# The merge of the odd heads of self blocks issued from ScalarE's queue, and all orders planned from new constants

## The reference

```python
# every block: normalise, modulate by the condition, compute, add to x (some through a gate)
L0: self attention (rope, block mask) -> cross attention (77 context tokens, mask) -> MLP 256-1024-256 (tanh gelu)
L1: cross attention (normalised and modulated context)
L2: self attention -> cross attention (normalised context) -> MLP (tanh gelu)
L3: self attention (rope) -> cross attention (rope) -> MLP (erf gelu)
# attention, 16 heads of 16: softmax(q k^T / 4) v, then the output projection
```

## Time and profile before

| | us |
|---|---|
| median of three executions | 2699.41 (2697.4 to 2700.83) |
| the profiled execution | 2701.83 |
| its span, first to last instruction | 2700.0 |
| PE busy | 2581.8 (96%) |
| DVE busy | 1747.8 (65%) |
| ACT busy | 1445.8 (54%) |
| POOL busy | 667.4 (25%) |
| mean granted clock of TensorE | 0.968 of full |

### The profile page before, as it was taken

One profiled execution on the slowest core, in us unless ns is written; L12 is line 12 of the kernel. 1 busy time (PEld: TensorE's weight loads), 2 busy tenths in 40 slices (PEclk: granted clock), 3 DMA queues, 4 the chain that ended last, 5 costly groups with the idle time before them and its releaser, 6 DMA issues.

```text
span 2700.0 us, 54860 instructions
## 1 busy us (share of the span) xinstructions
PE 2581.8 (96%) x19774; PEld 1869.2 (69%) x19774; DVE 1747.8 (65%) x4179; ACT 1445.8 (54%) x2421; POOL 667.4 (25%) x650
## 2 busy tenths in 40 slices
PE   7789999999999999989999999999999999999987
PEld 5557767677677766656777777777777777777765
DVE  4466666666665556677677767676677666766632
ACT  1235555544545555544566655556565656555642
POOL 2022222222221222212222222223323232324220
PEclk9799999999999988888999999999999999999989
DMA  6343423433433465554443434334335343434310
GB/s 206 101 146 123 128 94 120 133 96 100 139 105 108 132 200 167 167 174 142 132 146 112 144 109 135 119 124 134 118 103 177 101 139 106 144 100 136 105 62 18
DMA packets 297860, 340.55 MB, mean 126 GB/s; under 512 B 72954, under 2 KB 188506, under 8 KB 297020
## 3 DMA queue, kind: packets, MB, share of 16 engines
q1 hardware_dynamic: 264124, 286.68, 34.2%
q10 hardware_dynamic: 33280, 50.35, 5.1%
q0 software_dynamic: 192, 0.01, 0.0%
HBM read 203.42 MB, written 116.21 MB: 118 GB/s over the span
## 4 chain that ended last, share of the span: by engine, by line
PE 79%; DVE 10%; issue 3%; DMA 2%; SPq 1%; POOL 1%; ACT 1%; ACTq 0%; DVEq 0%; POOLq 0%
PE gen L1356 13%; PE gen L1365 12%; PE gen L1252 12%; PE gen L1218 11%; PE gen L1336 11%; PE score L1280 4%; PE score L1265 4%; PE score L1310 4%; DVE row_max L1691 4%; PE score L1294 3%; PE score L1316 3%; PE gen L1227 3%; DVE xhat L1605 1%; DVE x L1742 1%; POOL xnT L1550 1%
## 5 line engine op out<-in xcount | busy, mean ns | idle before, releaser
L1691 DVE TENSOR_REDUCE row_max<-score 128x4 f32<-128x1024 f32 (+1 forms) x640 | 650.6, 1045 | 210.4 <-PE score L1280 130.1
L1508 ACT ACTIVATE probs<-score 128x1024 f32<-128x1024 f32 (+1 forms) x576 | 570.9, 1026 | 369.6 <-PE score L1310 251.9
L1356 PE MATMUL gen<-xnT,w_w1M 128*128 128x256 f32 x1536 | 373.5, 392 | 3.1 <-ACT xnT L1446 2.9
L1365 PE MATMUL gen<-w_w2M,hT 128*128 128x256 f32 x1536 | 355.7, 385 | 3.0 <-ACT hT L1532 2.4
L1365 PEld LDWEIGHTS gen<-w_w2M,hT 128*128 128x128 f32 x1536 | 286.7, 191 | 65.1 <-issue 26.2
L1356 PEld LDWEIGHTS gen<-xnT,w_w1M 128*128 128x128 f32 x1536 | 284.9, 192 | 59.4 <-issue 7.5
L1550 POOL TENSOR_TENSOR xnT<-xnT,xhat 128x512 f32<-128x512 f32 x112 | 148.9, 1330 | 707.0 <-DVE xhat L1720 706.8
L1542 POOL TENSOR_TENSOR rstd<-var_eps,minus_half 128x2 f32<-128x2 f32 x160 | 115.7, 723 | 809.2 <-DVE var_eps L1599 809.0
L1532 ACT ACTIVATE hT<-gen,b_b 128x256 f32<-128x256 f32 x384 | 159.1, 472 | 179.0 <-PE gen L1356 178.0
L1446 ACT ACTIVATE xnT<-gen,mod_all 128x256 f32<-128x256 f32 x288 | 146.8, 569 | 153.7 <-PE gen L1227 151.2
L1336 PE MATMUL gen<-probs,v_self 128*32 128x256 f32 x3072 | 206.3, 386 | 0.5 <-ACT probs L1508 0.5
(11 more groups left out here) (160 smaller groups left out, 4050.4 us busy)
## 6 DMA issues: line engine op xcount, KB each, us to landing
q_stack<-parts_scratch SPq DMA_DIRECT2D x336, 256.0 KB
parts_scratch<-parts ACTq DMA_DIRECT2D x160, 256.0 KB, 2.5
parts_scratch<-parts SPq DMA_DIRECT2D x160, 256.0 KB, 2.3
k_self<-parts_scratch SPq DMA_DIRECT2D x144, 256.0 KB, 4.1
k_cross<-parts_scratch SPq DMA_DIRECT2D x192, 78.0 KB, 2.5
x_scratch<-x SPq DMA_DIRECT2D x48, 256.0 KB, 3.2
x_in<-x_scratch SPq DMA_DIRECT2D x48, 256.0 KB, 2.8
gate<-gates_scratch SPq DMA_DIRECT2D x80, 128.0 KB, 3.2
```

The costliest lines, as they stand in the source:

```text
L1356: mm = pe.matmul(buf[:, i * S:i * S + S], w["M"]["w1"][:, fc, col:col + P], xnT[s][:, fc, :], start=fc == 0, stop=fc == FC - 1)
L1365: mm = pe.matmul(buf[:, 0:D], hT[:, j, c * P:c * P + P], w["M"]["w2"][:, j, :], start=j == 0, stop=j == FFC - 1)
L1508: act.activation(probs[st.probs][0:keys, :, :], score[st.fill.buf][0:keys, :, :].rearrange("p a (r q) -> p (a r) q", r=2), ACT.Exp, bias=k ...
L1691: dve.tensor_reduce(dst, src, AX_X, ALU.max).then_inc(max_done[b], 1)
```

## The change

Two things. In self blocks too, `sh` becomes a step of ACT; the function that issued it from SP is gone. And 39 names instead of 33 have a bonus in `FIRST`, nearly all with other values; STAY is 4.1. Costs, rings, slots, arithmetic and the bytes moved stay as they are, and every engine's list is written anew by the same `run`.

```diff
-FIRST = {"S": 2.5, "ce": 15.3, "cl": 4.2, "dv": -3.6, "ex": -5.2, "ge": 15.3, "hi": 20.3, "ldc": 19.7, "ldg": 17.0, "ldx": 10.1, "lh": -6.3, "ln": -6.6, "lo": 8.1, "mr": 2.3, "mx": 5.7, "out": 3.8, "ph": -2.2, "pv": -6.6, "pw": 6.0, "qkv": -6.1, "res": -10.1, "rp": -1.8, "rt": -6.9, "sd": 9.4, "sg": -3.1, "sh": 10.2, "sm": 4.1, "stx": 6.3, "up": -0.1, "ve": -10.0, "xT": -2.5, "xb": -13.1, "xe": 8.4, "zq": 6.6}
-MARGIN, AGE, STAY = 1.38, 15.7, 4
+FIRST = {"S": 3.5, "ST": -0.1, "cT": -3.1, "ce": 17.4, "cl": 1.0, "dv": -1.2, "ex": 2.0, "ge": 23.1, "hi": 16.1, "ldc": 36.5, "ldg": 24.4, "ldx": 12.3, "lh": -24.9, "ll": -7.8, "ln": -18.0, "lo": -3.9, "mr": 3.0, "mx": -6.7, "nm": -10.1, "nx": 11.3, "out": 3.8, "ph": -2.2, "pv": -2.0, "pw": -5.3, "qkv": -6.0, "res": -16.5, "rp": 30.4, "rs": -2.3, "rt": -6.9, "sd": 23.1, "sg": 13.4, "sh": 8.7, "sm": -2.7, "stx": 16.5, "up": -0.1, "ve": -11.8, "xT": -2.5, "xb": -24.1, "xe": 8.4, "zq": 8.9}
+MARGIN, AGE, STAY = 1.38, 15.7, 4.1
...
-            placed.append(add("sh", h, "sp" if blk.whole else "act", [pv]))
+            placed.append(add("sh", h, "act", [pv]))
...
-                def place_heads(st):
-                    s, h, buf = st.slot, st.j, of(st, "pv", st.j).buf
-                    sp.wait_ge(*moved(of(st, "pv", h).fill))
-                    sp.dma_start(atT[s][1:P:2, h, :], oT[buf][1:P:2, 0, :]).then_inc(heads_placed[buf], 16)
...
-                    elif st.name == "sh":
-                        place_heads(st)
```

## The result

The changed kernel is slower: 2709.61 us in the median of nine executions (2694.7 to 2717.67), against 2695.43 (2685.19 to 2703.84) for the kernel before on the same chip. The medians lie 14.2 us apart; the ratio, which is estimated over all executions and so isn't exactly the quotient of the medians, is 1.0048, 95% interval [1.0033, 1.0063]. So 13 to 14 us are lost, where 13.5 were forecast to be won. The time lies inside the range of 2662 to 2711, near its upper end; it is rival (c)'s time. The profiled execution took 2717.55 us (span 2715.7, clock 0.967). PE is busy as long as before, 2582.6 us against 2581.8; what grew is its idle time, from 118.2 to 133.1 us. (The clock of the profiled execution before is 0.968.)

A forecast was written before the change was run, and what follows sets the result against it. PE (96% busy) was taken as the bound, with 160 us of idle time and lost clock to draw on. Terms -1 -2 -7 -4 -3 = -17, less a 3.5 discount, gave -13.5: 2686 us, range 2662 to 2711.

The forecast's parts named there:

- rival (c): L1 stretch: DVE's new list holds back `ln`, `res`, `lo`, `mx` behind maxima; slower, 2711 us; chance 22%.
- Part 1: Self blocks' `sh` issued from ACT: waits move to the gather, little gained; -1 us, between -3.5 and +8.
- Part 2, full stretches: 240 to 860 and 1320 to 2580 us: 10 fewer breaks in matmul runs; -2 us, 12 either way.
- Part 2, the L1 stretch: 860 to 1320 us: maxima earlier in DVE's list free score banks sooner; -7 us, bounds -30 and +20.
- Part 2, the start: Pipeline fill: a third of two stalls, 7.81 and 4.15 us, goes, with lost clock; -4 us, bounds -15 and +10.
- Part 2, the end: Last jobs: half a chance that `out` goes ahead of the previous job's `down`; -3 us, bounds -8 and +6.
- The discount: A quarter off the L1, start and end terms, since re-ordered lists can open new gaps; +3.5 us.

The follow-up runs named there:

- e1: The kernel before with only the 96 `sh` of self blocks moved from SP's list to ACT's, directly behind their `pv`: 2703.51 us, ratio 1.0015.
- e8: The kernel before with the last `out` ahead of job 62's two `down` and L2's first weight load 60 places later on SP: 2699.67 us, ratio 1.0002.
- e14: The changed kernel with DVE's job 17 statistics behind job 12's residual and SP's last MLP weight load behind job 52's loads: 2701.17 us, ratio 1.0004.

## Why the prediction was wrong

The sign was wrong, the size that of rival (c). Step by step:

**Part 1 (-1): right in what it described, its price not resolved.** The waits moved as said: L1119 grew by 124.8 us where L1125 had had 116.5. The landing is 2.0 us on ACT's queue. By time, e1's interval [0.9999, 1.0030] holds everything from -0.3 to +8 us; no wait of PE for an `ex` behind an `sh` was found. At one clock e1 stands at +4.8, inside the stated -3.5 to +8; the other three pairs don't repeat it. The Trainium skill's rule ("DMA: Bandwidth & Descriptors", "Issuing engines are not separate DMA queues") that another issuer saves only issue time fits: no gain was resolved in any of the four pairs.

**Part 2, full stretches (-2, within 12): this step failed, its bound just held.** By equal work the stretches of this step, with the edge from L2 to L3 that lies in the second, are 11.8 us longer (+7, -6, +6.6 and +4). L2 is 6 us shorter, since six waits of 0.66 to 0.69 us for row maxima and two for `xhat` (1.9 us) in the 8 idle us of the earlier trace rows are gone; L0 is 7 longer, mostly by the eight waits in front of score tiles (10.6 us), and L3 4 longer, in part by small gaps before `down`. The step took it that what other engines do is worth nothing there, because PE had only 14.7 idle us. That bounds a gain and not a loss. Breaks, on which it was built, hardly changed: 1776 changes of tiling in PE's list, 1774 before. How much of L0's +7 is real stays open, as said above; no edit took it away.

**Part 2, the L1 stretch (-7): this step failed, and it is the one that the experiments bear on.** It priced the stretch from 860 to 1320 as one, by PE's waits for maxima, and took half of a hoped-for gain. The maxima's three rows grew from 17.4 to 20.7 us. L1 and the edge before it are 5.8 us longer together: the edge is longer by 10.7, L1 shorter by 5. Rival (c) named the mechanism, a DVE list that holds back `res`, but put it in all sixteen jobs and behind maxima, at 4.8 us a job. The runs show it once, behind the context statistics of a job five ahead, in a wait of 5.9 us where it was 3.1, plus the clock. That rival (c)'s time came out is therefore luck in part. Which constant put the statistics in front is not shown: `res` went from -10.1 to -16.5 and `cl` from 4.2 to 1.0, but the walk with `res` alone put back to -10.1 still has them in front. The step's sum had no term for a level's edge, where the next jobs' first loads and the last residuals meet.

**Part 2, the start (-4): nothing.** The 7.81 us stall is 7.62 and the fill as long as before.

**Part 2, the end (-3): right.** The half chance came true: `out` of job 63 is ahead of the `down` of job 62, and the last `up` takes 7.17 instead of 9.65. It brings 2 us by equal work, and e8 says that so little isn't seen in the time.

**Missed: the edge from L2 to L3 (+6.6).** A weight load issued just ahead of the store and the loads of a job's keys. The prediction took nothing off or on for SP's order there. The profile shows this cause; that it costs time by itself no run shows, and with the order mended PE waits 3.36 us for the weights instead.

**The discount.** A quarter off for lists that fall differently was too little, and it could only shrink a gain. Of 160 us of idle time and clock the forecast took what could be won, and weighed what an order could lose only in its bounds.

## What to carry to other kernels

When all lists are planned anew, look at the places where one phase hands over to the next before summing terms over stretches: there steps of far-apart jobs stand next to each other, and one that waits for a load, put ahead of one whose data is there, made a wait of 5.9 us out of one of 3.1. In a planned list, keep a step that only prepares a later job behind the residual that frees a bank. A bulk load just ahead of a store that is waited for is worth avoiding too, though here its price in time is not shown. To mend a list, move single steps in the finished one: two moves gave back most, perhaps all, of what forty new constants had lost, while putting constants back changed places all over. And a bound from idle time bounds only what can be won: nearly idle-free stretches can still get longer.

## What the hardware showed

DVE and POOL got in each other's way beyond what a dependence says. The residual L1735, 0.426 us in the median, took 2.94 beside two POOL additions of 1.24 (the rows of the first edge above), and 1.25 before beside one. In e14, with the residual out of the way, the next DVE instruction beside the same two additions was stretched instead, 0.40 to 2.57 us:

```profile
884.80 2.57 DVE L1627 TENSOR_SCALAR ctx_in<-ctx_in,c_mean_var,c_rstd 77x256 f32<-77x256 f32 x1 [0.66 <-POOL c_rstd L1552]
```

with POOL beside it:

```profile
884.73 2.48 POOL L1581 TENSOR_TENSOR x<-x_in,late_gates 128x512 f32<-128x512 f32 x2
```

The Trainium skill ("SBUF — State Buffer", "SBUF: two separate sides") has the two engines share one pair of ports as a lock held for a whole instruction, with the other fully blocked, where the DVE instruction reads two inputs from SBUF (as the residual does) or runs in a mode that uses both of its ports. The rows agree, and add that DVE didn't get in between POOL's two additions either.

The low store at the second edge, 256 KB, took 8.2 us behind 2 MB of weights, where 2.4 is the median. The longest such store before, at 972.89, also stands behind 2 MB of weights (asked for at 969.42 and 969.93) and took 8.0 us, where 2.3 is the median. So a transfer asked for just behind a much larger one can wait for it. And the mean granted clock of one and the same kernel ranged from 0.965 to 0.973 over nine executions, 23 us apart, which is more than the whole effect studied.
